# Fused Perceiver layer on one core: the tail of the sparse attention and the head of the FFN, cut into token tiles

## The chip, the cores and the metric

The kernel runs on one NeuronCore of a Trainium2 chip. The metric is device time in microseconds (us) of one execution. The engines are PE (matrix products), DVE (vector), ACT (scalar and activation), POOL (GpSimd) and SP, which here only issues DMAs. Each runs its own instruction stream in order and waits for the others by semaphores.

## The reference, cut to what matters

512 token rows (8 batches of 64) of 512 features go through three residual layers: a cross-attention over 8 x 1601 context rows (unchanged here), a sparse attention and a ternary FFN.

```python
x = x + xattn(layernorm(x), ctx)                    # not touched
# sparse attention, y = layernorm(layernorm(x)) * gamma + beta
h = y @ W1.T                                        # [512, 128]
pair = relu(h[:, i] - h[:, j] + b1); pair = relu(pair @ W2.T + b2)
sim = pair @ W3.T + b3                              # [8, 64, 64], diagonal 0
mask = top 6 of every row of sim
q, k, v = split(y @ Wqkv.T + bqkv)                  # 32 heads of width 2
attn = softmax(q @ k.T / sqrt(2) + mask)
x = x + layernorm(x) + (attn @ v) @ Wout.T + bout
# FFN, w1 and w2 in {-1, 0, 1}
x = x + gelu(layernorm(x) @ w1.T + b1) @ w2.T + b2
```

## The kernel before, in words

`build` runs three stages one after the other: `attend` (to about 1842.6 us of the span), `sparse_attention` and `ternary_ffn`, each function ended for all engines by a barrier before the next one starts. Token rows lie 128 to a tile, so there are four token tiles. There is no planner in the two last stages: the order of work is the order in which each engine's function (`tensor`, `vector`, `scalar`, `gpsimd`, `sync`) is written.

In `sparse_attention` the features are turned (`yT`), `h` is made in one product, and then 32 pair items follow. For each unit of two items DVE subtracts (`first_layer`, L1842), ACT applies the ReLU (L1935), PE multiplies by `w2` (L1793), and the bias and ReLU of the result are done by DVE for even items (L1853) and by ACT for odd ones (L1948). Every four items PE makes the last layer (L1784), and SP spreads its rows into `sim2`. Behind the last item PE makes the token rows q, k, v for all four tiles (L1805, L1806), while DVE picks the six largest of every row and builds `mask`. PE turns the mask (L1813), one more product ranks the picked entries (L1817), and for each of the six ranks DVE makes a one-hot matrix (L1877) and PE gathers keys and values with it (L1824). DVE then does the softmax over the six ranks: maximum (L1895), exponent by ACT, weighting of the values, sum of the weights (L1907), and sum over the ranks (L1910), each sum or maximum one `tensor_reduce` over a strided view. The result `ao` is turned by PE (L1829), copied by ACT, multiplied by `wout` into four PSUM banks (L1833), and one DVE instruction adds the residual for all tiles (L1916).

In `ternary_ffn` (behind a barrier) SP loads `w2`; DVE takes the statistics of four tiles (L129, L131), POOL makes one reciprocal root for all four (L145), DVE norms four tiles (L137), PE turns 16 blocks by feature column (L160), ACT copies them out (L168), DVE rounds all of it to the high part (`x_hi`, L2059) and subtracts for the low part (`x_lo`, L2061). Only then do the hidden products start (L2025, L2026), 128 of them, with 128 output products (L2043, L2044) between them. `TileNorm` is a norm tile by tile that the stage before already uses.

Of the kernel before, what the change touches and what calls it, by code (L numbers as in the profile page):

```python
# [5 lines left out]
P = 128  # L6
F32 = mybir.dt.float32
# [3 lines left out]
ALU = mybir.AluOpType  # L11
# [1713 lines left out]
def sparse_attention(core, tail, x3, w1, w1_in):  # L1725
# [4 lines left out]
    with ExitStack() as stack:  # L1730
# [15 lines left out]
        pair1, pair2 = sb("pair1", [P, SLOTS, 2, 16, 64]), sb("pair2", [P, 8, 512])  # L1746
        simx = sb("simx", [P, 2, 512])
        picked, mask, top = sb("picked", [P, 4, 72]), sb("mask", [P, 4, P]), sb("top", [P, 4, 8])
        maskT, hot = sb("maskT", [P, 512], F32R), sb("hot", [P, TOPK, 512])
        prod = sb("prod_d", [P, TOPK, P, 2])  # L1750
        sc, prob = sb("sc_d", [P, TOPK, P]), sb("prob_d", [P, TOPK, P])
# [17 lines left out]
        def tensor():  # L1769
# [17 lines left out]

            for item in range(32):
# [8 lines left out]
                if item % 4 == 1 and item > 4:  # L1797
                    last_layer(item // 4 - 1)
            last_layer(7)

            PE.wait_ge(zeroed, 4)
            for t in range(4):
                out = s_ps[:, 1 + t // 2, 192 * (t % 2):192 * (t % 2) + 192]
                for c in range(4):
                    PE.matmul(out, yT[:, c, t * P:(t + 1) * P], wqkv[:, c, :], start=(c == 0), stop=False)  # L1805
                mm = PE.matmul(out, one_row[0:1, :], bqkv[0:1, :], start=False, stop=True)  # L1806
                if t % 2:
                    mm.then_inc(qkv_done, 1)

# [18 lines left out]
            for k in range(4):  # L1828
                mm = PE.transpose(sim_ps[0:64, k * P:(k + 1) * P], ao[:, k, :], ident[:])  # L1829
            mm.then_inc(ao_turned, 1)  # L1830
            PE.wait_ge(ao_moved, 1)
            for t in range(4):
                mm = PE.matmul(s_ps[:, t, :], aoT[:, t * P:(t + 1) * P], wout[:], start=True, stop=True)  # L1833
            mm.then_inc(out_done, 1)

        def vector():
# [160 lines left out]
def ternary_ffn(core, x3, w1, w1_in):  # L1997
    dram = core.dram
# [185 lines left out]
```

## Time and profile before

| | us |
|---|---|
| median of 3 runs (2038.59 to 2041.77) | 2040.56 |
| profiled execution, its own time | 2042.04 |
| its span in the trace | 2039.7 |
| PE busy of the span | 1889.2 (93%) |
| DVE busy | 1119.1 (55%) |
| ACT busy | 953.9 (47%) |
| POOL busy | 632.1 (31%) |

The trace's span is 2.3 us shorter than the execution's own time. Busy time is that of instructions, summed over the whole span; most of it belongs to the cross-attention. In a timeline row the first number is the start, the second the length of the merged group in us, then engine, line, operation, written tile and read tiles, shapes and count, and in brackets the idle time of the engine before it with what ended it. Tiles of the same name with a number are shown without it (`x` is `x3`, `pair` is `pair1` or `pair2`, `sim` is `sim2`). The granted clock is the share of PE's full clock.

### The profile page before, as it was taken

The numbers are of one execution on the slowest core, as the hardware profiler recorded it, in microseconds if no ns is written. First come the engines' busy times: TensorE is split into PE (matmuls) and PEld (weight loads), VectorE is DVE, ScalarE is ACT, GpSimd is POOL, SyncE is SP. The second block draws the span as 40 slices with busy tenths as digits, with TensorE's granted clock in tenths as the row PEclk, the third lists the DMA queues.
The fourth block names the chain that finished last, engine by engine and source line by source line (L and its number), as shares of the span: only waits on it lengthen the run. The fifth ranks groups of instructions, "written<-read, shape, count | busy, mean of one in ns | idle before, by whom it ended". The sixth has DMA issues, their size and how long they took to land. (4 is left out here: it accounts for less than half of the span.)

```text
span 2039.7 us, 30835 instructions
## 1 busy us (share of the span) xinstructions
PE 1889.2 (93%) x10105; PEld 1602.7 (79%) x10105; DVE 1119.1 (55%) x2977; ACT 953.9 (47%) x1938; POOL 632.1 (31%) x735
## 2 busy tenths in 40 slices
PE   3999999899999999999999999999999999884859
PEld 3778888788888888888888888888888887761337
DVE  6565465545564556455645565656565644435743
ACT  4554444545554555444545454545454544314611
POOL 3234553322232223333333343333333323002010
PEclk8999999999999999999999999999999999997969
DMA  6675444443544445344534453545444534452020
GB/s 196 205 248 169 120 134 152 136 132 111 173 155 127 122 158 174 98 128 152 174 109 145 139 170 109 151 139 164 114 147 140 149 111 135 133 196 83 3 83 21
DMA packets 225824, 280.66 MB, mean 138 GB/s; under 512 B 60346, under 2 KB 131259, under 8 KB 225667
## 3 DMA queue, kind: packets, MB, share of 16 engines
q1 hardware_dynamic: 215170, 277.84, 43.6%
q8 instruction: 82, 1.34, 0.3%
q10 hardware_dynamic: 8448, 0.43, 0.2%
q0 software_dynamic: 2048, 0.43, 0.1%
q14 instruction: 76, 0.61, 0.1%
HBM read 238.85 MB, written 39.22 MB: 136 GB/s over the span
## 5 line engine op out<-in xcount | busy, mean ns | idle before, releaser
L505 PE MATMUL kx_ps<-ctxT_hi,wk_hi 128*128 128x400 f32 (+1 forms) x1024 | 365.5, 357 | 16.2 <-DVE ctxT_lo L295 14.9
L507 PE MATMUL kx_ps<-ctxT_lo,wk_hi 128*128 128x400 f32 (+1 forms) x1024 | 355.7, 347 | 0.0
L509 PE MATMUL kx_ps<-ctxT_hi,wk_lo 128*128 128x400 f32 (+1 forms) x1024 | 355.1, 347 | 0.0
L588 PE MATMUL u_ps<-ctxN_hi,pt_hi 128*128 128x512 f32 (+1 forms) x832 | 341.7, 411 | 9.6 <-DVE pt_lo L826 9.4
L589 PE MATMUL u_ps<-ctxN_lo,pt_hi 128*128 128x512 f32 (+1 forms) x832 | 331.1, 398 | 0.0
L590 PE MATMUL u_ps<-ctxN_hi,pt_lo 128*128 128x512 f32 (+1 forms) x832 | 329.2, 396 | 0.0
L826 DVE TENSOR_TENSOR pt_lo<-t_ps,pt_hi 128x512 fp32r<-128x512 f32 (+1 forms) x256 | 144.5, 586 | 249.1 <-ACT pt_hi L1106 249.0
L1075 ACT ACTIVATE kx_hi<-kx_ps 128x400 fp32r<-128x400 f32 (+1 forms) x256 | 128.9, 504 | 318.7 <-PE kx_ps L509 315.4
L1106 ACT ACTIVATE pt_hi<-t_ps 128x512 fp32r<-128x512 f32 (+1 forms) x256 | 125.4, 522 | 263.0 <-PE t_ps L573 263.0
L753 DVE TENSOR_TENSOR kx_lo<-kx_ps,kx_hi 128x400 fp32r<-128x400 f32 (+1 forms) x256 | 146.6, 573 | 182.1 <-ACT sq L1077 181.5
L808 DVE CUSTOM_DVE_ANT_0 prob<-sc_ps,rstd_bc 128x400 f32<-128x400 f32 (+2 forms) x256 | 136.5, 570 | 142.8 <-PE sc_ps L561 142.8
L505 PEld LDWEIGHTS kx_ps<-ctxT_hi,wk_hi 128*128 128x128 f32 x1024 | 194.9, 190 | 22.1 <-DVE ctxT_lo L295 17.6
L588 PEld LDWEIGHTS u_ps<-ctxN_hi,pt_hi 128*128 128x128 f32 (+1 forms) x832 | 157.5, 189 | 49.4 <-DVE ctxN_lo L295 10.3
L507 PEld LDWEIGHTS kx_ps<-ctxT_lo,wk_hi 128*128 128x128 f32 x1024 | 194.1, 190 | 0.1
L509 PEld LDWEIGHTS kx_ps<-ctxT_hi,wk_lo 128*128 128x128 f32 x1024 | 193.4, 189 | 0.0
L590 PEld LDWEIGHTS u_ps<-ctxN_hi,pt_lo 128*128 128x128 f32 (+1 forms) x832 | 156.9, 189 | 38.3
L589 PEld LDWEIGHTS u_ps<-ctxN_lo,pt_hi 128*128 128x128 f32 (+1 forms) x832 | 157.8, 190 | 28.8
L1310 POOL TENSOR_TENSOR rstd_col<-var_col,minus_half 128x13 f32<-128x13 f32 x64 | 157.8, 2466 | 5.3
L1276 POOL TENSOR_SCALAR q_ve<-q_mv 128x1 f32<-128x1 f32 x64 | 15.2, 237 | 395.8 <-DVE q_mv L776 395.5
L573 PEld LDWEIGHTS t_ps<-ident,prob 128*128 128x128 f32 (+1 forms) x832 | 96.0, 141 | 50.6 <-issue 40.6
L573 PE MATMUL t_ps<-ident,prob 128*128 128x128 f32 (+1 forms) x832 | 126.4, 278 | 3.6 <-ACT prob L1228 1.9
L1077 ACT ACTIVATE sq<-kx_ps 128x400 f32<-128x400 f32 (+1 forms) x256 | 127.9, 500 | 0.0
(257 smaller groups left out, 3492.3 us busy)
## 6 DMA issues: line engine op xcount, KB each, us to landing
rstd_bc<-scratch_rstd SPq DMA_DIRECT2D x64, 804.0 KB, 6.0
stage<-in_ctx_t SPq DMA_DIRECT2D x96, 267.0 KB, 4.3
stage<-in_ctx_n SPq DMA_DIRECT2D x96, 256.0 KB, 6.1
wk_hi<-scratch_wk_s SPq DMA_DIRECT2D x56, 256.0 KB, 3.2
wk_lo<-scratch_wk_s SPq DMA_DIRECT2D x56, 256.0 KB, 3.7
wv_hi<-scratch_wv_s SPq DMA_DIRECT2D x56, 256.0 KB, 4.7
wv_lo<-scratch_wv_s SPq DMA_DIRECT2D x56, 256.0 KB, 5.7
scratch_own_rows<-out_sb SPq DMA_DIRECT2D x32, 256.0 KB, 2.7
```

The lines of the kernel that those rows point to most:

```text
L505: PE.matmul(kx_ps[:, j % 2, 0:w], wk_hi[:, g % 2, i, :], ctxT_hi[:, i, c0:c0 + w], start=(i == 0), stop=False)
L507: PE.matmul(kx_ps[:, j % 2, 0:w], wk_hi[:, g % 2, i, :], ctxT_lo[:, i, c0:c0 + w], start=False, stop=False)
L509: mm = PE.matmul(kx_ps[:, j % 2, 0:w], wk_lo[:, g % 2, i, :], ctxT_hi[:, i, c0:c0 + w], start=False, stop=(i == C - 1))
L573: mm = PE.transpose(t_ps[0:w, t % 2, k * P:(k + 1) * P], prob[:, y * P:y * P + w], ident[:])
L588: PE.matmul(u_ps[:], pt_hi[0:w, t % 2, cols], ctxN_hi[0:w, y, :], start=(y == 0), stop=False)
L589: PE.matmul(u_ps[:], pt_hi[0:w, t % 2, cols], ctxN_lo[0:w, y, :], start=False, stop=False)
L590: mm = PE.matmul(u_ps[:], pt_lo[0:w, t % 2, cols], ctxN_hi[0:w, y, :], start=False, stop=(y == NT - 1))
L753: V.tensor_tensor(kx_lo[:, n % 2, c0:c0 + w], kx_ps[:, u, 0:w], kx_hi[:, n % 2, c0:c0 + w].bitcast(F32), ALU.subtract).then_inc(kx_split, 1)
L808: V.tensor_tensor_reduce(prob[:, c0:c0 + v], sc_ps[:, j % 2, 0:v], rstd_bc[:, j, 0:v], 1.0, -3.0e38, ALU.mult, ALU.max, chunk_max[:, j:j + ...
L826: V.tensor_tensor(pt_lo[0:rows, t % 2, 0:cols], t_ps[0:rows, t % 2, 0:cols], pt_hi[0:rows, t % 2, 0:cols].bitcast(F32), ALU.subtract).then ...
L1075: A.activation(kx_hi[:, n % 2, c0:c0 + w], kx_ps[:, u, 0:w], ACTF.Copy).then_inc(kx_high, 1)
L1310: G.tensor_tensor(rstd_col[:], var_col[:], core.minus_half[:, 0:NT], ALU.pow).then_inc(pow_done, 1)
```

## The change

- In `tensor`, the token rows are made by a helper `token_rows(t, c)`. Eight of its sixteen calls (tiles 0 and 1) stand behind the even pair items 8 to 22, the other eight behind the last item.
- The three `tensor_reduce` instructions over six ranks become trees of `tensor_tensor`: ranks 0 to 2 with ranks 3 to 5, then the three halves together.
- `ao` is turned in two halves into two PSUM banks, copied in two halves, and each token tile of the output product signals by itself. DVE adds the residual and takes the statistics of a tile as it comes (`residual`), with the norm (`TileNorm`) of tile t behind the residual of tile t+1.
- The barrier between `sparse_attention` and `ternary_ffn` is gone; SP waits for `ao_done` before it loads `w2`. PE turns by token tile, ACT writes `x_hi` straight from PSUM, DVE subtracts `x_lo` from PSUM. `xn` and the norm's tiles are placed ahead of both stages, and the output has a tile of its own.
- `pair1` is released where it is placed, so later tiles share its memory. ACT sets `w3b` and `rankmat` ahead of its wait for `h`.

```diff
@@ -1785,6 +1787,16 @@
                                    pair2[:, (4 * group + c) % 8, :], start=True, stop=True)
                 mm.then_inc(sim_done, 1)
 
+            def token_rows(t, c):
+                out = s_ps[:, 1 + t // 2, 192 * (t % 2):192 * (t % 2) + 192]
+                PE.matmul(out, yT[:, c, t * P:(t + 1) * P], wqkv[:, c, :], start=(c == 0), stop=False)
+                if c == 3:
+                    if t == 0:
+                        PE.wait_ge(zeroed, 4)
+                    mm = PE.matmul(out, one_row[0:1, :], bqkv[0:1, :], start=False, stop=True)
+                    if t % 2:
+                        mm.then_inc(qkv_done, 1)
+
...
+                if 8 <= item < 24 and item % 2 == 0:
+                    token_rows((item - 8) // 8, (item - 8) // 2 % 4)
             last_layer(7)
 
-            PE.wait_ge(zeroed, 4)
-            for t in range(4):
-                out = s_ps[:, 1 + t // 2, 192 * (t % 2):192 * (t % 2) + 192]
+            for t in range(2, 4):
                 for c in range(4):
-                    PE.matmul(out, yT[:, c, t * P:(t + 1) * P], wqkv[:, c, :], start=(c == 0), stop=False)
-                mm = PE.matmul(out, one_row[0:1, :], bqkv[0:1, :], start=False, stop=True)
-                if t % 2:
-                    mm.then_inc(qkv_done, 1)
-
+                    token_rows(t, c)
...
@@ -1826,12 +1834,12 @@
                 mm.then_inc(gathered, 1)
             PE.wait_ge(ao_done, 1)
             for k in range(4):
-                mm = PE.transpose(sim_ps[0:64, k * P:(k + 1) * P], ao[:, k, :], ident[:])
-            mm.then_inc(ao_turned, 1)
-            PE.wait_ge(ao_moved, 1)
+                mm = PE.transpose((sim_ps, v_ps)[k // 2][0:64, k % 2 * P:(k % 2 + 1) * P], ao[:, k, :], ident[:])
+                if k % 2:
+                    mm.then_inc(ao_turned, 1)
             for t in range(4):
-                mm = PE.matmul(s_ps[:, t, :], aoT[:, t * P:(t + 1) * P], wout[:], start=True, stop=True)
-            mm.then_inc(out_done, 1)
+                PE.wait_ge(ao_moved, t // 2 + 1)
+                PE.matmul(s_ps[:, t, :], aoT[:, t * P:(t + 1) * P], wout[:], start=True, stop=True).then_inc(out_done, 1)
...
             V.wait_ge(multiplied, TOPK)
             V.tensor_tensor(sc[:], prod[:, :, :, 0], prod[:, :, :, 1], ALU.add).then_inc(s_step, 1)
             V.wait_ge(s_step, 1)
-            V.tensor_reduce(mx[:], sc[:].rearrange("p t x -> p x t"), AX.X, ALU.max).then_inc(s_step, 1)
+            V.tensor_tensor(half[:, :, 0:P], sc[:, 0:3, :], sc[:, 3:6, :], ALU.max).then_inc(s_step, 1)
             V.wait_ge(s_step, 2)
+            V.tensor_tensor(mx[:], half[:, 0, 0:P], half[:, 1, 0:P], ALU.max).then_inc(s_step, 1)
+            V.wait_ge(s_step, 3)
+            V.tensor_tensor(mx[:], mx[:], half[:, 2, 0:P], ALU.max).then_inc(s_step, 1)
+            V.wait_ge(s_step, 4)
             V.tensor_tensor(sc[:], sc[:], mx[:].unsqueeze(1).broadcast_to([P, TOPK, P]), ALU.subtract).then_inc(s_step, 1)
             V.wait_ge(s_exp, 1)
+            V.tensor_tensor(sc[:, 0:3, :], prob[:, 0:3, :], prob[:, 3:6, :], ALU.add).then_inc(s_step, 1)
...
+            V.wait_ge(s_step, 6)
+            V.tensor_tensor(sm[:], sc[:, 0, :], sc[:, 1, :], ALU.add).then_inc(s_step, 1)
...
-            V.tensor_reduce(sm[:], prob[:].rearrange("p t x -> p x t"), AX.X, ALU.add).then_inc(s_step, 1)
-            V.wait_ge(s_step, 6)
+            V.wait_ge(s_step, 8)
+            V.tensor_tensor(sm[:], sm[:], sc[:, 2, :], ALU.add).then_inc(s_step, 1)
+            rank = prod[:].rearrange("p t x d -> p t (x d)")
+            V.wait_ge(s_step, 9)
+            V.tensor_tensor(half[:], rank[:, 0:3, :], rank[:, 3:6, :], ALU.add).then_inc(s_step, 1)
+            V.wait_ge(s_step, 10)
             V.reciprocal(inv[:], sm[:]).then_inc(s_step, 1)
-            V.tensor_reduce(mixed_sb[:], prod[:].rearrange("p t x d -> p x d t"), AX.X, ALU.add).then_inc(s_step, 1)
-            V.wait_ge(s_step, 8)
+            mixed = mixed_sb[:].rearrange("p x d -> p (x d)")
+            V.wait_ge(s_step, 11)
+            V.tensor_tensor(mixed, half[:, 0, :], half[:, 1, :], ALU.add).then_inc(s_step, 1)
+            V.wait_ge(s_step, 13)
+            V.tensor_tensor(mixed, mixed, half[:, 2, :], ALU.add).then_inc(s_step, 1)
+            V.wait_ge(s_step, 14)
...
-            V.wait_ge(out_done, 1)
+            def residual(t):
+                V.wait_ge(out_done, t + 1)
+                V.tensor_tensor(x3[:, t, :], s_ps[:, t, :], xln[:, t, :], ALU.add).then_inc(x3_done, 1)
+                V.wait_ge(x3_done, t + 1)
+                norm3.vector_stats(t, x3)
+
             V.wait_ge(res_done, 2)
-            V.tensor_tensor(x3[:], s_ps[:], xln[:], ALU.add).then_inc(x3_done, 1)
-            V.wait_ge(x3_done, 1)
+            residual(0)
+            for t in range(4):
+                if t < 3:
+                    residual(t + 1)
+                norm3.vector_apply(t, x3, xn)
...
         def scalar():
             feat.scalar(1, yT, banks, "gamma", "beta")
             A.wait_ge(d_in, 16 * 7)
-            A.wait_ge(h_done, 1)
-            A.activation(hT[:], s_ps[:, 0, :], ACTF.Copy).then_inc(h_moved, 1)
-            A.activation(hTb[:], s_ps[:, 0, :], ACTF.Identity, bias=core.col("b1")).then_inc(h_moved, 1)
             A.wait_ge(zeroed, 1)
             for b2 in range(2):
                 hr = slice(64 * b2, 64 * b2 + 64)
                 A.activation(w3b[hr, b2:b2 + 1], core.col("w3")[hr, :], ACTF.Copy).then_inc(w3_set, 1)
             A.activation(rankmat[:], tail.rankmat[:], ACTF.Copy).then_inc(w3_set, 1)
+            A.wait_ge(h_done, 1)
+            A.activation(hT[:], s_ps[:, 0, :], ACTF.Copy).then_inc(h_moved, 1)
+            A.activation(hTb[:], s_ps[:, 0, :], ACTF.Identity, bias=core.col("b1")).then_inc(h_moved, 1)
...
-            A.wait_ge(s_step, 3)
+            A.wait_ge(s_step, 5)
             A.activation(prob[:], sc[:], ACTF.Exp, scale=2.0 ** -0.5).then_inc(s_exp, 1)
-            A.wait_ge(ao_turned, 1)
-            A.activation(aoT[:], sim_ps[0:64, :], ACTF.Copy).then_inc(ao_moved, 1)
+            for i in range(2):
+                A.wait_ge(ao_turned, i + 1)
+                A.activation(aoT[:, 2 * i * P:2 * (i + 1) * P], (sim_ps, v_ps)[i][0:64, 0:2 * P],
+                             ACTF.Copy).then_inc(ao_moved, 1)
...
+            for t in range(4):
+                norm3.gpsimd(t)
+
...
+            SP.wait_ge(ao_done, 1)
...
-            PE.wait_ge(norm.out_done, 12)
-            feat.tensor(2, xn, banks)
+            for t in range(4):
+                PE.wait_ge(norm3.out_done, t + 1)
+                after(PE, x_split, t - 1)
+                for c in range(4):
+                    mm = PE.transpose(banks[t % 2][:, c * P:(c + 1) * P], xn[:, t, c * P:(c + 1) * P], core.ident[:])
+                mm.then_inc(x_turned, 1)
             PE.wait_ge(w1_in, 16)
-            PE.wait_ge(x_split, 2)
-            PE.wait_ge(feat.moved, 12)
+            PE.wait_ge(x_split, 4)
...
-            norm.vector(2, x3, xn)
-            V.wait_ge(feat.moved, 12)
-            V.tensor_copy(x_hi[:], xT[:]).then_inc(x_split, 1)
-            V.wait_ge(x_split, 1)
-            V.tensor_tensor(x_lo[:], xT[:], x_hi[:].bitcast(F32), ALU.subtract).then_inc(x_split, 1)
+            for t in range(4):
+                V.wait_ge(x_high, t + 1)
+                cols = slice(t * P, (t + 1) * P)
+                V.tensor_tensor(x_lo[:, :, cols], banks[t % 2].rearrange("p (c s) -> p c s", c=4),
+                                x_hi[:, :, cols].bitcast(F32), ALU.subtract).then_inc(x_split, 1)
...
-            feat.scalar(2, xT, banks)
+            for t in range(4):
+                A.wait_ge(x_turned, t + 1)
+                A.activation(x_hi[:, :, t * P:(t + 1) * P], banks[t % 2].rearrange("p (c s) -> p c s", c=4),
+                             ACTF.Copy).then_inc(x_high, 1)
...
-            norm.gpsimd(2)
-            G.wait_ge(x_split, 2)
-            G.wait_ge(feat.turned, 12)
+            G.wait_ge(x_turned, 4)
...
-        sparse_attention(core, tail, x3, w1, w1_in)
-        nc.all_engine_barrier()
-        ternary_ffn(core, x3, w1, w1_in)
+        xn, norm3 = core.sb(stack, "xn_e", [P, 4, 512]), TileNorm(core, "e")
+        norm3.place(stack)
+        sparse_attention(core, tail, x3, xn, norm3, w1, w1_in)
+        ternary_ffn(core, x3, xn, norm3, w1, w1_in)
```

## Rows read from the trace of the kernel before

**Rows 1.** Busy time by stretch: each engine's us (instructions), granted clock, DMA share, GB/s.
```profile
1876.00:1899.64 23.64, 19.80 (x96) 4.06 (x96) 23.64 (x26) 22.72 (x29) 0.00 (x0) 1.00 0.01 3
...
1936.00:1948.00 12.00, 0.25 (x2) 0.21 (x3) 10.62 (x10) 0.84 (x1) 0.00 (x0) 0.60 0.00 0
...
1948.00:1974.00 26.00, 11.52 (x29) 5.75 (x27) 10.88 (x15) 4.23 (x6) 1.35 (x3) 0.57 0.45 162
...
1970.00:1972.00 2.00, 0.00 (x0) 0.00 (x0) 1.67 (x2) 1.55 (x2) 0.00 (x0) 1.00 1.05 402
...
1974.00:1979.40 5.40, 5.40 (x13) 4.23 (x14) 0.90 (x2) 0.69 (x1) 4.48 (x1) 0.50 0.00 0
...
1979.40:2034.90 55.50, 55.45 (x245) 45.54 (x243) 17.02 (x32) 10.35 (x15) 0.00 (x0) 1.00 0.00 0
```

**Rows 2.** Timeline from the end of the pair items to the mask's turning.
```profile
1919.32 1.57 PE L1805 MATMUL s_ps_d<-wqkv_d,yT_d 128*128 128x192 f32 x8
...
1924.67 0.61 DVE L1874 TENSOR_SCALAR mask<-picked 64x256 f32<-64x256 f32 x2
...
1927.38 0.66 PE L1813 MATMUL sim_ps_d<-ident,mask 128*128 128x128 f32 x4
```

**Rows 3.** Timeline of PE and DVE in the pair items.
```profile
1901.83 1.08 PE L1793 MATMUL b_ps_d<-pair,w_d 128*64 128x512 f32 x4 [0.50 <-ACT pair L1948]
...
1905.32 0.74 DVE L1853 TENSOR_SCALAR pair<-b_ps_d,cols 128x512 f32<-128x512 f32 x1
...
1906.11 1.08 PE L1793 MATMUL b_ps_d<-pair,w_d 128*64 128x512 f32 x4 [0.33 <-DVE pair L1853]
```

**Rows 4.** Timeline of DVE between the products and the weighted sums.
```profile
1936.19 0.96 DVE L1893 TENSOR_TENSOR sc_d<-prod_d 128x768 f32<-128x768 f32 x1
...
1937.18 1.45 DVE L1895 TENSOR_REDUCE mx_d<-sc_d 128x128 f32<-128x768 f32 x1
...
1938.66 0.96 DVE L1897 TENSOR_TENSOR sc_d<-sc_d,mx_d 128x768 f32<-128x768 f32 x1
...
1942.27 1.43 DVE L1907 TENSOR_REDUCE sm_d<-prob_d 128x128 f32<-128x768 f32 x1
...
1943.73 0.95 DVE L1909 RECIPROCAL inv_d<-sm_d 128x128 f32<-128x128 f32 x1
...
1944.60 2.64 DVE L1910 TENSOR_REDUCE mixed_d<-prod_d 128x256 f32<-128x1536 f32 x1
...
1947.27 0.42 DVE L1912 TENSOR_TENSOR ao_d<-mixed_d,inv_d 128x256 f32<-128x256 f32 x1
```

**Rows 5.** Timeline from the turned sums to the first statistics of the norm.
```profile
1947.75 1.06 PE L1829 MATMUL sim_ps_d<-ident,ao_d 128*64 128x128 f32 x4 [12.06 <-DVE ao_d L1912]
...
1948.85 0.59 ACT L1965 ACTIVATE aoT_d<-sim_ps_d 64x512 f32<-64x512 f32 x1 [8.36 <-PE sim_ps_d L1829]
...
1949.49 7.19 PE L1833 MATMUL s_ps_d<-wout_d,aoT_d 64*128 64x512 f32 x8 [0.68 <-ACT aoT_d L1965]
...
1956.72 2.29 DVE L1916 TENSOR_TENSOR x<-s_ps_d,xln_d 128x2048 f32<-128x2048 f32 x1 [9.02 <-PE s_ps_d L1833]
...
1959.41 0.69 DVE L129 BATCH_NORM_STATS2 stats_e<-x 128x6 f32<-128x512 f32 x1 [0.40 <-PEq L2117]
```

**Rows 6.** Timeline from the normed rows to the first hidden product.
```profile
1966.16 3.48 PE L160 MATMUL h_ps_e<-ident,xn_e 128*128 128x128 f32 x16 [9.48 <-DVE xn_e L137]
...
1967.31 0.60 ACT L168 ACTIVATE xT_e<-h_ps_e 128x512 f32<-128x512 f32 x1 [17.87 <-PE h_ps_e L160]
...
1973.96 0.76 PE L2025 MATMUL h_ps_e<-xhi_e,w1t 128*128 128x512 f32 x1 [4.32 <-DVE xlo_e L2061]
```

**Rows 7.** Timeline of DVE in the tile norms of the stage before.
```profile
1825.39 0.69 DVE L1604 BATCH_NORM_STATS2 tstats_d<-x 128x6 f32<-128x512 f32 x1
...
1841.45 0.18 DVE L1606 BATCH_NORM_AGGREGATE tmv_d<-tstats_d 128x2 f32<-128x6 f32 x1
...
1842.63 0.55 DVE L1611 TENSOR_SCALAR y_d<-xln_d,tmv_d,trstd_d 128x512 f32<-128x512 f32 x1 [1.00 <-POOL trstd_d L1619]
```

More of the change, by code:

```diff
@@ L1722, in products, with sparse_attention @@
             mm.then_inc(self.part_done, 1)
-def sparse_attention(core, tail, x3, w1, w1_in):
+def sparse_attention(core, tail, x3, xn, norm3, w1, w1_in):
     nc, dram, ident = core.nc, core.dram, core.ident
@@ L1745, in sparse_attention @@
         SLOTS, AHEAD = 6, 3
-        pair1, pair2 = sb("pair1", [P, SLOTS, 2, 16, 64]), sb("pair2", [P, 8, 512])
-        simx = sb("simx", [P, 2, 512])
+        pair2, simx = sb("pair2", [P, 8, 512]), sb("simx", [P, 2, 512])
         picked, mask, top = sb("picked", [P, 4, 72]), sb("mask", [P, 4, P]), sb("top", [P, 4, 8])
+        with ExitStack() as inner:
+            pair1 = core.sb(inner, "pair1", [P, SLOTS, 2, 16, 64])
         maskT, hot = sb("maskT", [P, 512], F32R), sb("hot", [P, TOPK, 512])
         prod = sb("prod_d", [P, TOPK, P, 2])
+        half = sb("half_d", [P, 3, 2 * P])
         sc, prob = sb("sc_d", [P, TOPK, P]), sb("prob_d", [P, TOPK, P])
@@ L1994, in sparse_attention, with ternary_ffn @@
         sync()
-def ternary_ffn(core, x3, w1, w1_in):
+def ternary_ffn(core, x3, xn, norm3, w1, w1_in):
     dram = core.dram
     PE, V, A, G, SP = core.PE, core.DVE, core.ACT, core.POOL, core.SP
-    sem, norm, feat = core.sem, core.norm, core.features
+    sem = core.sem
     RING = 3
@@ L2008, in ternary_ffn @@
         w2 = sb("w2t", [P, 16, 512], F32R)
-        xn, xT = sb("xn_e", [P, 4, 512]), sb("xT_e", [P, 4, 512])
+        out = sb("out_e", [P, 4, 512])
         x_hi, x_lo = sb("xhi_e", [P, 4, 512], F32R), sb("xlo_e", [P, 4, 512], F32R)
@@ L2012, in ternary_ffn @@
         h_hi, h_lo = sb("hhi_e", [P, RING, 512], F32R), sb("hlo_e", [P, RING, 512], F32R)
-        norm.place(stack, "e")
         banks = [h_ps[:, 0, :], h_ps[:, 1, :]]
         w2_in = [sem(f"w2_in{q}") for q in range(4)]
-        x_split, hidden_done, gelu_done = sem("x_split"), sem("hidden_done"), sem("gelu_done")
+        x_turned, x_high, x_split, hidden_done, gelu_done = sem("x_turned"), sem("x_high"), sem("x_split"), sem("hidden_done"), sem("gelu_done")
         h_high, h_split, part_done = sem("h_high"), sem("h_split"), sem("ffn_part")
@@ L2069, in vector @@
             for t in range(4):
-                V.tensor_tensor(xT[:, t, :], o_ps[:, t, :], xn[:, t, :], ALU.add).then_inc(out_ready, 1)
+                V.tensor_tensor(out[:, t, :], o_ps[:, t, :], xn[:, t, :], ALU.add).then_inc(out_ready, 1)
         def scalar():
-            feat.scalar(2, xT, banks)
+            for t in range(4):
+                A.wait_ge(x_turned, t + 1)
+                A.activation(x_hi[:, :, t * P:(t + 1) * P], banks[t % 2].rearrange("p (c s) -> p c s", c=4),
+                             ACTF.Copy).then_inc(x_high, 1)
             for f in range(16):
@@ L2091, in sync @@
                 SP.wait_ge(out_ready, t + 1)
-                SP.dma_start(dram["out"][t * P:(t + 1) * P, :], xT[:, t, :]).then_inc(stored, 16)
+                SP.dma_start(dram["out"][t * P:(t + 1) * P, :], out[:, t, :]).then_inc(stored, 16)
             SP.wait_ge(stored, 64)
```

## The prediction

> **What bounds the kernel now.** I read the busy time by stretch first, then the timeline of the last 120 us, then the chain of waits backwards from the end. The change touches nothing before 1842 us, so only this tail counts. In the pair items [rows 1] DVE is busy for all of the 23.64 us looked at, PE for 19.80: DVE sets the pace, and PE has 3.84 us free there, in short waits behind DVE and ACT [rows 3]. Behind the pair items no engine is full. From 1936 to 1948 us it is DVE alone (10.62 of 12 us busy, PE 0.25), and from 1948 to 1974 PE is busy for 11.52, DVE for 10.88 of 26 us: they take turns. From 1974 to 2035 PE is full. So the time at stake is the serial stretch from 1919 to 1974 us, 54.6 us, and the pair items as the place where work could be hidden or could hurt.
>
> **1. Token rows between the pair items.** Before, four tiles of rows take PE from 1919.32 to 1927.38, 2.015 us each, and the mask's turning starts right behind them, though DVE's mask is ready at 1924.67 + 0.61 = 1925.28 [rows 2]. With two tiles behind the items PE is free at about 1923.35; what is late next is the mask itself, so the turning starts at 1925.35 instead of 1927.38: **-2.0**. All later steps hang on it one to one. The sums for k and v come out of PSUM earlier than before, so ACT's copies hold nobody up.
>
> The two tiles moved are 4.03 us of PE work in eight pieces, six of about 0.4 us and two of about 0.9 (the bias product comes with every fourth). They stand behind items of which one is followed by PE's wait of 0.50 us, another by the 0.33 us wait [rows 3]. Sixteen items take about the 23.6 us of [rows 1]; per four items (5.9 us) PE waits 0.83 us and gets 0.75 more work, plus the bias once in sixteen items' worth. DVE's own slack helps: the item started at 1906.11 is done by 1907.2, and DVE comes to it only half a period behind 1905.32, at about 1908.2. So nearly all is hidden; I charge **+0.2**. If the cover were gone, it would be all 4.0.
>
> ACT's `w3b` and `rankmat` copies move into its wait for h: the first subtraction of DVE waits for `hTb` either way, so 0.
>
> **2. Trees for the six ranks.** Starts in [rows 4] give what each reduce costs DVE: maximum 1938.66 - 1937.18 = 1.48, sum of weights 1.46, weighted sum 1947.27 - 1944.60 = 2.67, together 5.61. The adds: 768 elements take 0.96 and 256 take 0.42, so 0.15 us plus 1.05 ns per element, which also gives 2.30 for the 2048 of [rows 5], measured 2.29. Then 384 elements are 0.555, 128 are 0.285, and a step that waits for the one before adds 0.03, one that doesn't saves 0.08 (1943.73 + 0.95 against 1944.60). Maximum: 0.585 + 2 x 0.315 = 1.22. Sum of weights, woven between the two products: 0.475 + 2 x 0.20 = 0.88. Weighted sum: 0.88 for 768, then the reciprocal (as before), then 2 x 0.45 = 0.90: 1.78. Together 3.87: **-1.7**. Bounds: every one of the nine adds 0.1 slower than the line says gives -0.8; the reads with fewer strides could make it -2.0. I take the line, since it meets three rows.
> The Trainium skill, "VectorE: DVE Perf Modes", section Rules for kernel authors, says that chained vector work is to be judged by the number of operations, not of semaphores; nine operations in place of three would then speak against the trees. By that rule alone, with its fixed part at the 0.15 of the row, the edit would cost about 0.9; but the same page has the reduce among the slowest operations, and [rows 4] show it at 2.64 for 1536 elements where the line would give 1.76. The row decides.
>
> **3. `ao` in two halves.** Before, turning starts at 1947.75 and the output product at 1949.49, 1.74 later (1.10 turning, 0.64 copy) [rows 5]. Two blocks instead of four are about 0.75 until ACT sees them, a half copy about 0.4: **-0.6** (0 to -0.8).
>
> **4. Output product to the first hidden product.** Before: 1973.96 - 1949.49 = 24.47 us [rows 5, 6]. After, counted from the start of the output product, T:
> - PE's four tiles: the last reaches DVE at 7.23 as before, each takes 1.70, so 2.13, 3.83, 5.53, 7.23.
> - DVE per tile: add 0.69 (the line at 512), statistics 0.69, aggregate 0.18 [rows 7], 1.56 together, and the norm 0.55, less 0.07 overlap: 2.04. Residual 0 runs 2.13 to 3.69, residual 1 3.83 to 5.39, norm 0 to 5.89, residual 2 to 7.45, norm 1 to 7.95, residual 3 to 9.51, norm 2 to 10.0. POOL's root comes back 1842.63 - 1841.45 = 1.18 after an aggregate starts [rows 7]; the last starts at 9.41, so norm 3 runs from 10.59 to 11.14. Only this last round trip is uncovered (0.6 us).
> - PE turns tiles 0 and 1 meanwhile. Tile 2 needs a bank that `x_lo` of tile 0 frees, and that stands behind norm 3 in DVE's queue: this is the wait that the change adds. `x_lo`(0) 11.1 to 11.76; PE turns tile 2 and ACT sees it 1967.31 - 1966.16 = 1.15 later [rows 6], 12.95; tile 3 follows 0.85 behind, 13.8; ACT copies it in 0.60 to 14.4; `x_lo`(3) 0.69 to 15.15; first hidden product at 15.2. Behind the waiting PE instruction stand only the hidden products; what waits for them is everything.
> So 24.47 - 15.2 = **-9.3**. In it lie the barrier's 0.40 [rows 5], the whole `x_hi` cast by DVE, and most of one 2.29 us addition and one such subtraction. Bounds: -7.5, if waits at each tile cost 0.2 more on both engines; -10.5, if PE runs at full clock here.
>
> `w2` is now loaded from `ao_done` on, over a stretch with no other transfer, and before the first output product needs it; POOL's 4.5 us addition for the end starts with tile 3's turning instead of with the hidden products, while DVE does two subtractions. Both 0; the cover of the latter is the whole hidden loop.
>
> **5. The clock of the hidden products.** Before, 13 instructions in 5.40 us at granted clock 0.50 (1.2 GHz), 0.42 each, then 245 in 55.5 at 1.00 (2.4 GHz), 0.227 each [rows 1]. PE had waited 4.32 us for `x_lo` [rows 6]; at 1970 it was still at 1.00 after the 16 turnings. After the change PE's break before the hidden products is only 1.4 us, but its work before is in four pieces. From 0 to -2.7 if they start at full clock, up to +1.3 if the low clock lasts half as long again. I take 0, because the pieces before are as short as those before which they started low.
>
> **Sum.** -2.0 + 0.2 - 1.7 - 0.6 - 9.3 + 0 = -13.4. The profiled execution took 2042.04 us, which is its span of 2039.7 and 2.3 around it; 2042.04 - 13.4 = 2028.6. It lies 1.48 above the median of the runs, so the median should come to 2027.1.
>
> **Rivals.**
> - *PE becomes the bound between the pair items.* For it: PE is busy for 84% of the loop, with 0.83 us of waits per four items against 0.75 added. Against it: DVE's and ACT's slack of up to a microsecond behind each item. All 4.0 us back: -9.6, 2031. Chance 0.08.
> - *PE falls to half clock before the gathering.* PE now stands for 2 us before the mask's turning, and then works in short pieces; at 1936 to 1948 us it fell to half clock in an idle stretch (mean 0.60) [rows 1]. The 48 gathering products would then start at about double length, some 2 us lost before the clock is back, 5.7 at worst: 2029 to 2032.8. Against it: PE still works for about 1.2 of the 4.7 us in question, while in the row of the fall it had 0.25 of 12. Chance 0.12. The Trainium skill, "TensorE: Matmul & The Clock Gate", section Why this matters for your kernels, warns that idle gaps between bursts bring the clock back to half; the fall in the 1936 to 1948 stretch agrees, and whether this gap suffices no row before shows.
> - *The tiles don't overlap as counted.* Each tile adds waits on three engines, and one late root or bank shifts all behind it. The steps then give -6 in place of -9.3: 2030.4. Chance 0.11.
> - *Full clock from the first hidden product*: a further -2.7, 2024.4. Chance 0.08.
> - *Slower than before: the hidden products stay at half clock.* One mechanism: PE comes to them from a stretch of small pieces and is not granted full clock for long. Each instruction at half clock costs 0.42 - 0.227 = 0.19 us, so beyond 70 more such instructions of the 256 the gain is used up; with 100 more, 2033 + 13 = 2046. Against it: in the same position full clock came after 13. Chance 0.02.
> - *The change does nothing*, because the waits of DVE's queue order make it as serial as before: chance 0.02, 2040.
>
> **How the numbers follow.** The forecast has 0.57, with an own range of 2025 to 2029. The range for 8 in 10 takes in the partial losses and the early clock: 2023.5 to 2032.5. A measurement of this kernel tells 0.2% (4 us) from no change, so faster means below 2036.5: all but the two last rivals and a remainder, 0.95; same 0.03; slower 0.02.
>
> **What would show it.** Right, if the mask's turning starts within 0.1 us of the mask's end, PE's rows L1805 stand between pair items and the first item to the last take no more than 0.5 us longer; if `ao` is finished 1.7 us earlier against the last multiplication; if the output product's start lies about 15 us (not 24.5) before the first hidden product, with DVE nearly without a gap from residual 1 to norm 2; and if the hidden loop with the output products keeps its 61 us within 3. Wrong, if the pair items stretch by several microseconds, if the gathering shows clock 0.5, or if DVE waits for `out_done` or for the root at every tile.

## The result

The changed kernel took 2031.07 us (median of 5 runs, 2024.33 to 2032.81) against 2040.56 before (5 runs, 2038.59 to 2042.28). The ratio is 0.9947, with a 95% interval of 0.9929 to 0.9966: 11 us less, between 7 and 14.5. A second set of six runs gave 2028.8 us and 0.9946 (0.9933 to 0.9959). Forecast were 2027.1 us, in a range of 2023.5 to 2032.5; the narrower range of 2025 to 2029 misses the first median and holds the second.

The profiled execution, the slowest of the five, took 2032.81 us, its span 2031.5. The span is 8.2 us shorter than that of before. To see where these come from, I cut both traces at the same nine events. All times are differences of starts in the timelines. "First instruction over the scores" is DVE's addition that follows the six products of the gathering (L1893 before, L1901 now):

| from | to | before | after | difference | forecast |
|---|---|---|---|---|---|
| start of the span | turning of y | 1856.53 | 1858.19 | +1.66 | 0 |
| turning of y | first pair subtraction | 9.69 | 11.50 | +1.81 | 0 |
| first pair subtraction | last PE group of the items | 52.11 | 52.50 | +0.39 | +0.2 |
| last PE group | mask's turning | 9.05 | 7.01 | -2.04 | -2.0 |
| mask's turning | first gathering product | 2.72 | 2.72 | 0 | 0 |
| first gathering product | first instruction over the scores | 6.09 | 7.45 | +1.36 | 0 |
| first instruction over the scores | turning of `ao` | 11.56 | 9.78 | -1.78 | -1.7 |
| turning of `ao` | output product | 1.74 | 1.10 | -0.64 | -0.6 |
| output product | first hidden product | 24.47 | 15.35 | -9.12 | -9.3 |
| first hidden product | end of the span | 65.74 | 65.90 | +0.16 | 0 |

The five edited steps give -13.2 us; three other rows, where no cost was forecast, take back 4.8 us in this execution. The last row hides two more that cancel, told at the end of this section. The timeline after, from the last token rows to the gathering, answers to [rows 2]:

```profile
1925.20 1.57 PE L1792 MATMUL s_ps_d<-wqkv_d,yT_d 128*128 128x192 f32 x8
...
1928.53 0.61 DVE L1882 TENSOR_SCALAR mask<-picked 64x256 f32<-64x256 f32 x2
...
1929.20 0.66 PE L1821 MATMUL sim_ps_d<-ident,mask 128*128 128x128 f32 x4 [1.91 <-DVE mask L1882]
...
1930.54 0.50 PE L1825 MATMUL v_ps_d<-maskT,rankmat_r 128*128 128x512 f32 x1 [0.69 <-ACT maskT L1992]
...
1931.92 5.17 PE L1832 MATMUL s_ps_d<-kv_d,hot 128*128 128x128 f32 x32 [0.88 <-DVE hot L1885]
```

PE has its rows done at 1927.3 and waits 1.91 us for DVE's mask, where before it didn't wait. Then the gathering: it had clock 1.00 before and runs at 0.80 now. The columns are those of [rows 1]; first two stretches of before, then the same ones and three more of after:

```profile
1861.00:1866.00 5.00, 3.67 (x8) 1.44 (x8) 0.00 (x0) 1.08 (x3) 4.92 (x2) 1.00 1.03 395
...
1930.00:1936.00 6.00, 5.60 (x48) 5.43 (x48) 5.05 (x11) 0.00 (x0) 0.00 (x0) 1.00 0.00 0
```

```profile
1863.00:1869.00 6.00, 5.38 (x8) 2.09 (x8) 0.00 (x0) 1.04 (x5) 4.99 (x2) 0.71 1.04 391
...
1889.00:1912.00 23.00, 23.00 (x112) 6.56 (x106) 22.77 (x23) 21.96 (x28) 0.00 (x0) 1.00 0.02 4
...
1932.00:1939.00 7.00, 6.88 (x48) 6.68 (x48) 4.78 (x11) 0.00 (x0) 0.00 (x0) 0.80 0.00 0
...
1950.00:1966.00 16.00, 11.65 (x27) 5.98 (x26) 10.51 (x20) 4.22 (x7) 5.58 (x9) 0.50 0.73 262
...
1965.60:1969.00 3.40, 3.40 (x8) 2.73 (x9) 0.00 (x0) 0.43 (x1) 3.12 (x1) 0.51 0.03 5
```

The 48 gathering products, the first of them at half clock, keep PE busy for 6.88 us instead of 5.60, and DVE waits for them. The product for h (first line of each) is the same eight instructions, at 1.00 before and 0.71 now. In the pair items, with the added rows between them (second line), PE is busy for the whole 23.00 us and DVE for 22.77. Once DVE waits for PE there:

```profile
1903.18 0.75 DVE L1861 TENSOR_SCALAR pair<-b_ps_d,cols 128x512 f32<-128x512 f32 x1 [0.23 <-PE b_ps_d L1805]
```

The trees, which answer to [rows 4]:

```profile
1939.37 0.96 DVE L1901 TENSOR_TENSOR sc_d<-prod_d 128x768 f32<-128x768 f32 x1
...
1940.36 0.56 DVE L1903 TENSOR_TENSOR half_d<-sc_d 128x384 f32<-128x384 f32 x1
...
1940.96 0.29 DVE L1905 TENSOR_TENSOR mx_d<-half_d 128x128 f32<-128x128 f32 x1
...
1945.89 0.28 DVE L1923 TENSOR_TENSOR sm_d<-sm_d,sc_d 128x128 f32<-128x128 f32 x1
...
1946.09 0.95 DVE L1926 TENSOR_TENSOR half_d<-prod_d 128x768 f32<-128x768 f32 x1
...
1946.96 0.94 DVE L1928 RECIPROCAL inv_d<-sm_d 128x128 f32<-128x128 f32 x1
...
1948.67 0.42 DVE L1935 TENSOR_TENSOR ao_d<-mixed_d,inv_d 128x256 f32<-128x256 f32 x1
```

And the stretch of tiles, answering to [rows 5 to 7]: output product, residual, norm, turning, split, first hidden product.

```profile
1949.15 0.64 PE L1837 MATMUL sim_ps_d<-ident,ao_d 128*64 128x128 f32 x2 [10.28 <-DVE ao_d L1935]
...
1950.25 7.19 PE L1842 MATMUL s_ps_d<-wout_d,aoT_d 64*128 64x512 f32 x8
...
1952.43 0.69 DVE L1939 TENSOR_TENSOR x<-s_ps_d,xln_d 128x512 f32<-128x512 f32 x1 [3.34 <-PE s_ps_d L1842]
...
1954.07 0.69 DVE L1939 TENSOR_TENSOR x<-s_ps_d,xln_d 128x512 f32<-128x512 f32 x1
...
1957.38 1.97 PE L2070 MATMUL h_ps_e<-ident,xn_e 128*128 128x128 f32 x8
...
1960.86 0.55 DVE L1611 TENSOR_SCALAR xn_e<-x,tmv_e,trstd_e 128x512 f32<-128x512 f32 x1 [0.77 <-POOL trstd_e L1619]
...
1961.32 1.28 DVE L2099 TENSOR_TENSOR xlo_e<-h_ps_e,xhi_e 128x512 fp32r<-128x512 f32 x2
...
1962.15 1.94 PE L2070 MATMUL h_ps_e<-ident,xn_e 128*128 128x128 f32 x8 [2.81 <-DVE xlo_e L2099]
...
1964.76 0.69 DVE L2099 TENSOR_TENSOR xlo_e<-h_ps_e,xhi_e 128x512 fp32r<-128x512 f32 x1 [0.16 <-ACT xhi_e L2114]
...
1965.60 0.76 PE L2061 MATMUL h_ps_e<-xhi_e,w1t 128*128 128x512 f32 x1 [1.50 <-DVE xlo_e L2099]
```

PE's turning of the third tile starts at 1962.15, behind the first `x_lo` (the two are one row of 1.28 us), though its norm was done at 1960.1: this is the wait for a bank that the change adds. The last root is waited for 0.77 us. Else DVE works back to back from the first residual to the second `x_lo`; then it waits 1.30 us for the third tile's `x_hi`.

The loop of hidden and output products, at full clock in both, comes out slower after: [rows 1] have 245 PE instructions in 55.5 us, 0.2265 us each; the first fence here is a stretch of after by the same view, 228 in 52.6, 0.2307 each, and from the view by groups (busy time, mean ns) the line of its hidden products with `x_hi`, at 398 ns. The second has the same two of the kernel "old head" below, whose last stage has its tiles declared as before: 233 in 52.8, 0.2266, and 389 ns.

```profile
1974.00:2026.60 52.60, 52.60 (x228) 42.45 (x226) 15.39 (x28) 8.94 (x13) 0.00 (x0) 1.00 0.00 0
...
L2061 PE MATMUL h_ps_e<-xhi_e,w1t 128*128 128x512 f32 x52 | 20.7, 398 | 0.0
```

```profile
1975.00:2027.80 52.80, 52.78 (x233) 43.36 (x231) 15.96 (x29) 9.66 (x14) 0.00 (x0) 1.00 0.00 0
...
L2050 PE MATMUL h_ps_e<-xhi_e,w1t 128*128 128x512 f32 x52 | 20.2, 389 | 0.0
```

The 398 is the largest of the four groups of after (398, 393, 393, 391; all four are 389 in old head); the time per instruction is the fairer measure. Over the 248 instructions left at full clock its difference, 0.0042 us, makes 1.0 us. It doesn't show in the table because the loop ran at half clock for 3.4 us after and 5.4 us before, which gives back 1.0.

### The profile page after: what moved, and what is told of

It is laid out like the page before. It is cut to its first block and busy times, and to the rows that moved or that the text cites. A ratio compares the mean times of both kernels' runs of the same rounds, so it can differ in the third digit from the quotient of the medians.

```text
span 2031.5 us, 30842 instructions
## 1 busy us (share of the span) xinstructions
PE 1894.2 (93%) x10105; PEld 1605.2 (79%) x10105; DVE 1117.8 (55%) x2988; ACT 953.2 (47%) x1939; POOL 636.1 (31%) x741
## 5 line engine op out<-in xcount | busy, mean ns | idle before, releaser
L505 PE MATMUL kx_ps<-ctxT_hi,wk_hi 128*128 128x400 f32 (+1 forms) x1024 | 366.3, 358 | 16.5 <-DVE ctxT_lo L295 15.2
```

Source lines behind the costliest of these rows:

```text
L505: PE.matmul(kx_ps[:, j % 2, 0:w], wk_hi[:, g % 2, i, :], ctxT_hi[:, i, c0:c0 + w], start=(i == 0), stop=False)
```

## The experiments

Each kernel is the changed one with the edit shown. "Tail" is the time from the turning of y to the end of the span; medians are of 5 to 12 runs each, and each set is compared with runs of the kernel before on the same chip (medians 2039.57 to 2041.56). The last three columns are from the first trace of each kernel; two kernels have a second trace, told in their sections.

| kernel | median us | ratio to before, 95% interval | tail | gathering to scores | output product to hidden |
|---|---|---|---|---|---|
| before | 2040.56 | 1 | 183.2 | 6.09 | 24.47 |
| changed | 2031.07 | 0.9947 (0.9929 to 0.9966) | 173.3 | 7.45 | 15.35 |
| changed, again | 2028.80 | 0.9946 (0.9933 to 0.9959) | 172.5 | 7.52 | 15.33 |
| rows behind | 2030.63 | 0.9957 (0.9941 to 0.9972) | 173.4 | 6.10 | 15.34 |
| reduces | 2032.13 | 0.9952 (0.9935 to 0.9968) | 174.2 | 7.62 | 15.33 |
| old head | 2037.70 | 0.9995 (0.9982 to 1.0008) | 180.3 | 7.52 | 24.76 |
| barrier | 2031.62 | 0.9951 (0.9935 to 0.9968) | 174.5 | 7.55 | 17.52 |
| four banks | 2028.51 | 0.9946 (0.9928 to 0.9963) | 171.0 | 7.67 | 13.83 |
| mask wait filled | 2029.67 | 0.9945 (0.9928 to 0.9961) | 172.1 | 7.72 | 15.34 |
| filled to the gathering | 2028.09 | 0.9945 (0.9931 to 0.9959) | 170.9 | 6.09 | 15.34 |
| filled to the end | 2023.98 | 0.9923 (0.9910 to 0.9936) | 168.9 | 6.10 | 15.84 |
| filled, four banks, swap | 2026.38 | 0.9928 (0.9915 to 0.9941) | 168.3 | 6.09 | 13.20 |

The medians scatter by more than most of these edits are worth. The turning of y, before which no edit changes an instruction, started between 1852.4 and 1858.5 us in the 14 traces. So for edits of 1 to 2 us the stage times of the traces decide, which repeat within 0.15 us for the same code and clock; the medians decide only for the large ones.

**The changed kernel again** (no edit).

> The changed kernel once more, for a second profile and five more times beside the others. Theory (steps as counted, rest is PE's clock and scatter ahead of the tail): the steps of the change reappear within 0.2 us in this trace (pair items +0.4, token rows -2.0, trees with the weighting -1.8, turning of ao -0.6, output product to first hidden product 15.3 instead of 24.5), while the start of the tail (1858.2 us in the first profile, 1856.5 before), the product for h (5.4 us at half clock, 3.7 before) and the gathering (7.45 us from its first product to the sum, 6.1 before) may come out differently. Rival (the change itself slows the stages around it): start of the tail, product for h and gathering all come out as in the first profile. Median: theory 2029 to 2031, rival 2031 to 2032.

The edited steps reappeared within 0.03 us (52.50, 7.01, 9.77, 1.11, 15.33). The start of the tail (1853.22) and the product for h (turning of y to the first pair 9.81 instead of 11.50) did not: they scatter. The gathering did, 7.52. Here the clock fell already before the mask's turning, and the stretch from there to the first gathering product took 3.47 us instead of 2.72. So two of the three losses of the first trace are scatter, and the third looks like the change's own.

**All token rows behind the items again.**

```diff
-                if 8 <= item < 24 and item % 2 == 0:
-                    token_rows((item - 8) // 8, (item - 8) // 2 % 4)
...
-            for t in range(2, 4):
+            for t in range(4):
                 for c in range(4):
                     token_rows(t, c)
```

> All token rows behind the last pair item as before, everything else changed. Theory (clock falls before the gathering because PE now stands for 2 us): the pair items lose their 0.4 us, the mask's turning starts 2.0 us later, but PE has no such pause and the gathering is back to 6.1 us from 7.45, so part 1 is worth only about 0.3 us: median within 0.5 us of the changed kernel's. Rival (the fall is chance and has nothing to do with the pause): the trace of this kernel shows it as often as that of the changed one, and the median is 1.6 us above the changed kernel's.

> The kernel with all token rows behind the items, a second trace. Theory (the pause takes the clock from the gathering): 6.1 us again from the gathering to the sum over pairs. Rival (it is chance): 7.5.

The two traces gave 6.10 and 6.09 us for the gathering, at full clock; last PE group to mask's turning 9.06 in both, pair items 52.05 and 52.06. The stretch in its first trace:

```profile
1932.00:1938.00 6.00, 5.60 (x48) 5.43 (x48) 5.05 (x12) 0.00 (x0) 0.00 (x0) 1.00 0.00 0
```

Interleaving the rows is then worth 2.05 - 0.45 - 1.4 = 0.2 us against the first trace of the changed kernel, where I had counted 1.8. In its second trace, where the clock also cost 0.75 us ahead of the gathering, it is a loss of 0.6. The medians (2030.6 against 2031.1 and 2028.8) can't tell such differences.

**Fillings ahead of the gathering.** Products of `w1` with itself into a free bank, read by nobody.

```diff
+            PE.wait_ge(w1_in, 16)
+            for _ in range(8):
+                PE.matmul(b_ps[:, 0, :], w1[:, 0, 0:P], w1[:, 0, :], start=True, stop=True)
             PE.wait_ge(topk_step, 12)
```

> Only the pause of 1.9 us before the mask's turning is filled, with eight products of w1 into a free bank; nothing reads them. Theory (the pause is what takes the clock from the gathering): first gathering product to the sum over pairs 6.1 us as before instead of 7.5, everything else as in the changed kernel, -1.4 us. Rival (the short pieces between the mask's turning and the gathering do it): 7.5 us again, no gain.

> The kernel with only the pause before the mask's turning filled, a second trace. If 7.5 us for the gathering again, the fill in that place is worth nothing; if 6.1, this kernel stands at the edge and it depends on the execution.

First trace 7.72, second 6.09. So with the pause of 1.9 us filled the clock still fell in one trace of two: what is left between mask and gathering (the mask's turning of 0.65 us and one ranking product of 0.49 us, with a wait behind each) can be enough. My theory that the pause alone does it is refuted by the first trace. With 2 and 3 more products in those two waits:

> The pause before the mask's turning and the two short ones up to the gathering are filled (8, 2 and 3 products), nothing else. Theory (the short pieces around the ranking take the clock as much as the pause did): gathering 6.1 us, -1.4 against the changed kernel, 2027 to 2029. Rival (the clock falls there whatever PE does): 7.5.

6.09 us, clock 1.00. The two kernels below that fill the same places, and more behind them, have 6.10 and 6.09. Three traces can't show that this always holds, but the rival, that the clock falls whatever PE does, is out.

**Fillings to the end.** 8, 2, 3 products as above, 42 behind the gathering, 1 behind the turning of `ao`, 2 behind each output tile, 3, 4, 10 and 5 behind the four turned tiles.

> The changed kernel with products of w1 with itself into a free PSUM bank wherever PE waits behind the pair items (8 before the mask's turning, 2 and 3 around the ranking, 42 behind the gathering, 1 behind the turning of ao, 2 behind every output tile, 3, 4, 10 and 5 behind the four turned tiles); nothing reads them. Theory (the missing gain is PE's clock): granted clock stays at 1.00 from the pair items to the end; the gathering takes 6.1 us instead of 7.45 (-1.4), the output product 3.6 us instead of 7.2 so that the residuals start about 0.9 us earlier, turnings 0.4 us shorter each on the path (-0.8), the hidden products start at full clock (-1.3 to -2.7): together -4 to -6 us against the changed kernel, 2025 to 2027. Rival (the clock is not what costs here, or the added products stand in the way of what comes next): same or slower.

The clock stays at 1.00 from the pair items to the hidden products. Columns as in [rows 1]: gathering, softmax, turning of `ao` to the hidden products:

```profile
1925.70:1931.80 6.10, 6.10 (x51) 6.00 (x52) 5.12 (x12) 0.00 (x0) 0.00 (x0) 1.00 0.01 3
...
1931.80:1941.50 9.70, 9.06 (x40) 7.13 (x38) 8.58 (x15) 0.85 (x1) 0.00 (x0) 1.00 0.00 0
...
1941.50:1958.00 16.50, 14.83 (x59) 8.54 (x59) 10.39 (x21) 3.60 (x7) 4.89 (x9) 1.00 0.71 254
```

The gathering took 6.10 us, the step from the turning of `ao` to the output product 0.87 instead of 1.10, and the hidden loop with the last additions 64.3 instead of 65.9. Output product to first hidden product, however, took 15.84 us, not less. The first residual began 1.23 us behind the output product instead of 2.18, but ten of the added products stood ahead of the last turning:

```profile
1943.68 0.69 DVE L1950 TENSOR_TENSOR x<-s_ps_d,xln_d 128x512 f32<-128x512 f32 x1 [2.16 <-PE s_ps_d L1852]
...
1953.40 0.63 PE L2081 MATMUL h_ps_e<-ident,xn_e 128*128 128x128 f32 x4 [1.52 <-DVE xlo_e L2112]
...
1953.79 2.56 PE L2084 MATMUL o_ps_e<-w1t 128*128 128x512 f32 x10
...
1956.18 0.60 PE L2081 MATMUL h_ps_e<-ident,xn_e 128*128 128x128 f32 x4
...
1958.29 0.47 PE L2072 MATMUL h_ps_e<-xhi_e,w1t 128*128 128x512 f32 x1 [0.35 <-DVE xlo_e L2112]
```

The norm of that tile was done at 1952.7 and its bank free at about 1953.85; from then to 1956.18 the added products held the turning up. Even so the ratio, 0.9923, is below that of the changed kernel: the slowest of its six runs took 2026.82 us, and of the changed kernel's eleven only two were below that (2024.33 and 2026.48).

**Trees undone.** The three `tensor_reduce` of before in place of the nine instructions, with the waits renumbered.

```diff
-            V.tensor_tensor(half[:, :, 0:P], sc[:, 0:3, :], sc[:, 3:6, :], ALU.max).then_inc(s_step, 1)
...
+            V.tensor_reduce(mx[:], sc[:].rearrange("p t x -> p x t"), AX.X, ALU.max).then_inc(s_step, 1)
...
```

> The three reduces over the six ranks are back in place of the nine additions and maxima, everything else changed. Theory (150 ns plus 1.05 ns per element for each added instruction, as the trace showed): from the first instruction over the scores to the turning of ao 11.56 us again instead of 9.78, so +1.8 us against the changed kernel. Rival (DVE's time counts less, since PE waits in either case for something else): under 1 us.

Scores to turning of `ao`: 11.58 us against 9.78, so 1.8, all of it on the path.

**Old head.** Parts 1 to 3 kept; residual in one piece, barrier, norm, turning and split as before.

```diff
+            V.wait_ge(out_done, 4)
             V.wait_ge(res_done, 2)
-            residual(0)
...
+            V.tensor_tensor(x3[:], s_ps[:], xln[:], ALU.add).then_inc(x3_done, 1)
...
+        nc.all_engine_barrier()
```

> The token rows between the items, the trees and the halves of ao stay; residual, barrier, norm, split and the first hidden product are as before. Theory: the stretch from the output product to the first hidden product is 24.4 us again (15.3 in the changed kernel), so the median is 9.1 us above the changed kernel's, about 2039 to 2040, 1 to 4 us below before. Rival (part of the stretch's gain is given back in the hidden loop, by the clock or by POOL's addition beside it): less than 7 us above.

24.76 us from the output product to the first hidden one, so the tiles and the removed barrier together are worth 9.4 there; the median is 6.6 to 8.9 us above the changed kernel's two, the ratio 0.9995 against 0.9947 and 0.9946, which is about 10 us. The other three parts alone can't be told from no change. From the first hidden product to the end it took 65.2 us, the changed kernel 65.9 and 66.0, although that had the shorter stretch at half clock (3.4 us against 4.2): this is the slower product of the section above. From 8.4 to 56 us behind the first hidden product, PE starts one every 0.230 us in all twelve traces with the new head, every 0.226 in this one and 0.2245 in that of before.

The 16 turnings are the same ones as before, but here they ran at half clock and did not end it; it was 0.50 up to 1971.7:

```profile
1959.42 3.77 PE L160 MATMUL h_ps_e<-ident,xn_e 128*128 128x128 f32 x16 [9.48 <-DVE xn_e L137]
```

**Barrier.** Only this line:

```diff
         sparse_attention(core, tail, x3, xn, norm3, w1, w1_in)
+        nc.all_engine_barrier()
```

> The changed kernel with the barrier between its two stages put back; tiles, splits and trees stay. Theory (what the barrier costs is the overlap of the first two turnings with the norm, not its own 0.4 us): the turning of tile 0 starts behind the last norm, 4.5 us later than now, and the first hidden product about 2.2 us later, 17.5 us behind the output product. Rival (a barrier costs its own 0.4 us): 15.8.

17.52 us, as worked out. PE waits at the barrier (PEq) until all norms are done, turns two tiles, waits 0.65 us for a bank and turns the other two:

```profile
1958.64 1.94 PE L2070 MATMUL h_ps_e<-ident,xn_e 128*128 128x128 f32 x8 [4.28 <-PEq L2159]
...
1961.23 1.94 PE L2070 MATMUL h_ps_e<-ident,xn_e 128*128 128x128 f32 x8 [0.65 <-DVE xlo_e L2099]
...
1964.68 0.77 PE L2061 MATMUL h_ps_e<-xhi_e,w1t 128*128 128x512 f32 x1 [1.50 <-DVE xlo_e L2099]
```

**Four banks.**

```diff
-        banks = [h_ps[:, 0, :], h_ps[:, 1, :]]
+        banks = [h_ps[:, 0, :], h_ps[:, 1, :], h_ps[:, 2, :], o_ps[:, 0, :]]
...
-                after(PE, x_split, t - 1)
```

> The four token tiles are turned into four PSUM banks, so that the turning of tiles 2 and 3 no longer waits for x_lo of tiles 0 and 1. Theory (the wait for the bank is what the last part of the stretch consists of): the turning of tile 3 starts with its norm, about 1.6 us earlier, and the first hidden product 1.0 to 1.6 us earlier: output product to first hidden product 13.7 to 14.3 us instead of 15.35. Rival (DVE's four subtractions in a row are the bound): less than 0.7 us.

13.83 us, 1.5 less. Each turning now waits for nothing but DVE's norm of its tile, and three subtractions run in one piece:

```profile
1954.28 1.11 PE L2069 MATMUL h_ps_e<-ident,xn_e 128*128 128x128 f32 x4 [0.81 <-DVE xn_e L1611]
...
1955.60 1.12 PE L2069 MATMUL o_ps_e<-ident,xn_e 128*128 128x128 f32 x4 [0.20 <-DVE xn_e L1611]
...
1955.46 1.88 DVE L2098 TENSOR_TENSOR xlo_e<-h_ps_e,xhi_e 128x512 fp32r<-128x512 f32 x3
...
1957.39 0.69 DVE L2098 TENSOR_TENSOR xlo_e<-o_ps_e,xhi_e 128x512 fp32r<-128x512 f32 x1
...
1958.22 0.77 PE L2061 MATMUL h_ps_e<-xhi_e,w1t 128*128 128x512 f32 x1 [1.51 <-DVE xlo_e L2098]
```

**All of it.** Four banks, fillings (5, 5, 3, 6 behind the turned tiles), and `x_lo` of tile 0 in the wait for the last root.

```diff
             for t in range(4):
+                if t == 1:
+                    norm3.vector_apply(3, x3, xn)
                 V.wait_ge(x_high, t + 1)
```

> Four banks, products of w1 with itself in all of PE's waits behind the pair items (as in the kernel with fillings, but 5, 5, 3 and 6 behind the four turned tiles instead of 3, 4, 10 and 5), and DVE's x_lo of tile 0 put into its wait for the last root. Theory (clock and bank are the two things left in this stretch): gathering 6.1, ao's turning to the output product 0.9, output product to first hidden product 12.0 to 12.8 us (15.35 in the changed kernel, 15.8 in the first filled one, where ten products stood ahead of the last turning), hidden loop 59.5 instead of 61: 3 us faster than the first filled kernel, about 2020.5 to 2021.5. Rival (DVE's subtractions bound the end of the stretch): 13.5 us or more, 2022.

13.20 us, neither the 12.0 to 12.8 of the theory nor the rival's 13.5, and the median, 2026.38, misses both (2020.5 to 2021.5, and 2022). Why the stage stopped at 13.20 wasn't followed up. The tail is the shortest of all, 168.3 us, though this trace has the product for h at half clock (turning of y to the first pair 11.8 us). Against the first filled kernel the ratios (0.9928 and 0.9923) are not to be told apart; in the traces the stage is 2.6 us shorter. Both ratios are about 2 in a thousand below the changed kernel's, though the intervals overlap with its own.

## Why the prediction came out as it did

The edited steps came out as counted; two costs beside them, one given a small chance and the other none, took back 2.4 us.

- *Pair items* (+0.2): measured +0.39. DVE did stop: its step for the even items comes every 2.93 us, once it came after 3.24 (a wait of 0.23 us for PE at 1903) and a few times some hundredths late. The rival that PE becomes the bound is right so far as PE was busy all 23.00 us of its row; but DVE kept its pace, and the price was 0.4 instead of 4.0.
- *Token rows* (-2.0): -2.04; the mask is late next, as said.
- *Trees* (-1.7): -1.78, and 1.80 when undone. The line of 0.15 us plus 1.05 ns per element gave 0.555 for 384 elements (0.56 measured), 0.285 for 128 (0.28 to 0.29), 0.96 for 768 (0.95). The Trainium skill's rule in "VectorE: DVE Perf Modes", section Rules for kernel authors, to count operations, would have made it +0.9; the trace has it at -1.78. The remark of the same section that `tensor_reduce` is the slowest operation agrees with it.
- *Halves of `ao`* (-0.6): -0.64. No run undoes this part by itself.
- *Tiles* (-9.3): -9.12. The schedule held event by event: the first residual started 2.18 us behind the output product (2.13 worked out), the last norm ended at 11.16 (11.14), the first hidden product came at 15.35 (15.2).
- *Clock of the hidden products* (0): -1.0 in this trace, inside the range given. The half clock lasted 3.4 us here and in the second trace, 5.4 before, but from 2.9 to 5.2 us over the ten traces with the new head and nothing filled in behind the gathering. With one trace of before, this difference is within the scatter.
- *What was missing, first*: the first gathering products at half clock. I had it as a rival with "some 2 us" and a chance of 0.12, and the gathering at clock 0.5 as a sign of being wrong. It cost 1.4 to 1.6 us, and it came in all six traces that had the 1.9 us pause unfilled (7.45 to 7.67), and in none of the three without the moved rows. I had argued against it with PE's share of work in the pause, from a single row that showed a fall; no row told how much work holds the clock. The step that failed is therefore the cover of part 1: PE's wait wasn't free, and of the 1.8 us counted for the part 0 to 0.2 were left in the five traces where the clock fell only at the gathering.
- *What was missing, second*: 1.0 us in the loop that I had left at 0, each product 1.8% longer at the same clock. Every kernel with the new head has it, the old head hasn't. The difference that I know of for these products is where their operands lie (`xn` and 160 bytes of norm tiles are now declared ahead of them). That the placement is the cause wasn't tried and stays open.
- With both the sum is -13.2 + 1.4 + 1.0 = -10.8, and the ratio of the runs says -10.8 (7 to 14.5). That they meet to a tenth is luck: the sum leaves out what the hidden loop's clock won in the trace, with which it is -11.8, and the interval holds either. It is also luck that the loop's slower product and its clock cancel in the trace, so that its length seems untouched.
- In the rival of the hidden products that stay at half clock, "2033 + 13" doesn't follow from the terms: 100 more instructions at 0.19 us on 2027 give the same 2046.
- The other two losses of the profiled execution, the start of the tail (+1.66) and the product for h (+1.81), are in PE's code that the change leaves alone (two small copies of ACT moved into its wait for h), and all but went away in the second trace. The same long product for h stands in both traces with the rows behind the items and in the last filled one. They are why one span shows only 8.2.

## What to carry to other kernels

Work taken out of PE's queue ahead of a wait leaves a pause, and what PE does behind it may then run at half clock, as here in six traces of six: when a step is moved, look at what PE does just after the gap. When several engines take turns over tiles, writing down the schedule tile by tile from durations of rows gives the new length within some tenths of a microsecond, including the one wait that the cut adds (here the bank). Here every product of a loop that was left alone got 1.8% longer, for a reason that isn't isolated, so such a loop is worth a look as well. When identical code ahead of the change scatters by 6 us, compare stage by stage in several traces rather than the totals of single runs.

## What the runs showed of the hardware

- The gathering's length fell into two groups, 6.09 to 6.10 at full clock (seven traces) and 7.45 to 7.72 with part of it at 1.2 GHz (seven traces). The product for h likewise: turning of y to the first pair subtraction was 9.62 to 9.81 us in ten traces and 11.37 to 11.83 in four, with the same code.
- PE busy for 7.2 us with the 64-row output product did not bring full clock in any of the twelve traces where it started at half. Sixteen turnings of 128 rows did in the trace of before (3.5 us, 1.00 at 1970, [rows 1]), but the same sixteen did not in that of the old head (3.8 us, 0.50 up to 1971.7).
- Products that nobody reads kept the clock at 1.00 from the mask's turning to the hidden products, 35 us in which PE otherwise fell to 0.5.
- The same product of 512 columns took 0.230 us from start to start at full clock in the twelve traces with the new head and 0.2245 to 0.226 in the two with the old one. The tiles' placement differs between them; that it is the cause isn't shown.
